# Causal attention of row b placed between the experts of row b-1, and the loop over rows written out

## The reference, cut to what matters

```python
xn = layernorm(x)
# s: causal attention 1, 16 heads of 8
pressure = where(causal, -10000, q1 @ k1.T * hd**-0.5)
attn = 1 - tanh((pressure - threshold) / tau)**2
attn = attn / (sum(attn) + 1e-6)
s = (attn @ v1) @ Wo1.T
# g: attention 2 (softmax, not causal) with residual, then a mixture of 8 experts, top 2, and a shared one
h = rmsnorm(xn, norm1_w);  X = xn + (softmax(q2 @ k2.T * scale) @ v2) @ wo
h2 = rmsnorm(X, norm2_w)
combine = top2 softmax weights of softmax(h2 @ router_w)
moe = swiglu(h2, shared) + sum_e combine[e] * swiglu(h2, expert e)
out = x + s * silu(X + moe)
```

## Time and profile before

| what | value |
|---|---|
| median of 3 runs | 1255.82 us (1254.42 to 1259.35) |
| the profiled execution, its own time | 1256.73 us |
| its span | 1255.0 us |
| PE busy | 1120.9 us, 89% of the span |
| DVE, ACT, POOL busy | 840.3, 649.3, 338.4 us |
| mean granted clock of PE | 0.946 of full |
| first score product | 77.8 us |

### The profile page before, as it was taken

The page is one execution under the profiler, slowest core; times in us unless marked ns, Lnnn a source line. Parts: engine busy times, 40 slices in busy tenths (PEclk is TensorE's granted clock), DMA queues, the critical chain, the costliest instruction groups (busy, mean ns, idle before and its releaser), DMA issues.

```text
span 1255.0 us, 21105 instructions
## 1 busy us (share of the span) xinstructions
PE 1120.9 (89%) x7112; PEld 480.4 (38%) x7112; DVE 840.3 (67%) x1692; ACT 649.3 (52%) x873; POOL 338.4 (27%) x177
## 2 busy tenths in 40 slices
PE   2479999899998899899998999989999899998998
PEld 1112454234541354314543245422464234542365
DVE  6365976569657686576865688655976558656673
ACT  4039821597117861278513883149721597218841
POOL 5400443015420334103341035310543014420013
PEclk8559999799998999989998999989999799999999
DMA  5520432003411135102341033410342104400020
GB/s 173 99 35 2 77 103 42 28 2 77 118 26 28 24 55 134 22 17 44 70 107 28 2 63 99 58 28 2 77 109 35 29 4 74 130 15 18 1 69 8
DMA packets 67970, 66.86 MB, mean 53 GB/s; under 512 B 7760, under 2 KB 59216, under 8 KB 67728
## 3 DMA queue, kind: packets, MB, share of 16 engines
q1 hardware_dynamic: 65088, 61.26, 22.9%
q10 hardware_dynamic: 2768, 4.06, 0.9%
HBM read 50.22 MB, written 14.81 MB: 52 GB/s over the span
## 4 chain that ended last, share of the span: by engine, by line
PE 65%; issue 10%; ACT 10%; DVE 9%; DMA 3%; SPq 2%; POOL 1%; ACTq 1%; DVEq 0%; POOLq 0%
PE M L906 12%; PE O L980 10%; PE O L964 10%; PE S L996 8%; PE S L998 5%; PE S L997 5%; PE S L939 4%; ACT PT L525 4%; DVE PT L676 4%; DVE nmax L639 3%; PE M L1069 1%; SPq L321 1%; PE M L899 1%; PE M L893 1%; PE M L918 1%
## 5 line engine op out<-in xcount | busy, mean ns | idle before, releaser
L525 ACT ACTIVATE PT<-S 128x1024 f32<-128x1024 f32 (+1 forms) x448 | 421.1, 973 | 122.7 <-PE S L939 119.6
L639 DVE TENSOR_REDUCE nmax<-M 128x1 f32<-128x512 f32 x512 | 338.3, 688 | 200.1 <-PE M L906 196.6
L676 DVE SCALAR_TENSOR_TENSOR PT<-PT 128x768 f32<-128x768 f32 (+1 forms) x192 | 215.7, 1173 | 95.9 <-ACT PT L525 95.6
L906 PE MATMUL M<-stackK,stackQ 48*128 48x512 bf16 x512 | 214.5, 434 | 60.9 <-DMA stackK<-scrK 27.5
L964 PE MATMUL O<-PT,V 128*12 128x256 f32 (+3 forms) x2816 | 250.7, 437 | 0.0
L559 ACT ACTIVATE PT<-S 128x1024 f32<-128x1024 f32 x72 | 73.9, 1026 | 313.0 <-PE S L998 313.0
L400 POOL TENSOR_TENSOR split<-split,parts 128x512 f32<-128x512 f32 x32 | 93.1, 2909 | 489.3 <-ACT parts L486 489.3
L415 POOL TENSOR_TENSOR PT<-PT,CB 128x1024 f32<-128x1024 f32 x56 | 132.8, 2373 | 336.3 <-DMA CB<-scrC 171.1
L939 PE MATMUL S<-stackQ,stackK 64*128 64x512 bf16 (+3 forms) x1024 | 205.6, 362 | 18.8 <-DMA stackQ<-mTZ 9.3
L906 PEld LDWEIGHTS M<-stackK,stackQ 48*128 48x128 bf16 x512 | 46.9, 95 | 299.3 <-issue 175.6
L980 PE MATMUL O<-PT,wdn 128*128 128x512 f32 x288 | 151.5, 625 | 0.0
(11 more groups left out here) (174 smaller groups left out, 932.7 us busy)
## 6 DMA issues: line engine op xcount, KB each, us to landing
CB<-scrC SPq DMA_DIRECT2D x64, 256.0 KB, 5.4
stackQ<-scrQ SPq DMA_DIRECT2D x192, 64.0 KB
stackK<-scrK SPq DMA_DIRECT2D x192, 64.0 KB
scrQ<-parts SPq DMA_DIRECT2D x16, 384.0 KB, 4.5
scrK<-parts SPq DMA_DIRECT2D x16, 384.0 KB, 8.3
PT<-in_w_gu ACTq DMA_DIRECT2D x2, 1152.0 KB, 8.2
xin<-in_x SPq DMA_DIRECT2D x8, 256.0 KB, 2.9
xres<-in_x SPq DMA_DIRECT2D x8, 256.0 KB, 3.3
```

The lines of the kernel that those rows point to most:

```text
L525: a.activation(PT[:, n % SLOTS, 2 * q * w:2 * q * w + 2 * w].rearrange("p (r n) -> p r n", r=2), S[k][:, :].rearrange("p (r n) -> p r n", ...
L639: v.tensor_reduce(nmax[:, h % 2, h // 2, t:t + 1], M[k][:, :], AX.X, ALU.max, negate=True).then_inc(m_read[k], 1)
L676: v.scalar_tensor_tensor(p, p, 1.0, p, ALU.subtract, ALU.mult).then_inc(weighed, 1)
L906: t_.matmul(M[k][:, :], stack["Q2"][a:a + ROW_ADD, hp, t * 128:t * 128 + 128], stack["K2"][a:a + ROW_ADD, hp, :], start=True, stop=True).t ...
```

## The change

The program of each row is written out, with no machine loop. One list, ITEMS, gives the order: stage 1 of row b (units 0 to 15), experts 0 to 4 of row b-1, causal units 16 to 19 of row b, experts 5 to 8 of row b-1, units 20 to 23, the gate `G` of row b-1, units 24 to 27. It runs for b from -1 to 8; what belongs to no row is left out, so row 0 has no experts in between and row 7's experts stand alone at the end. BEHIND says which V product (V) or second expert product (D) follows each item. The last two V products of a row lie in units 0 and 1 of the next, its attention-1 output (`oT1`, `ctxT1`, `proj1`) in units 10 to 14.

The maxima X cover head pairs 0 to 2 now, and a run W covers pair 3, in units 0 and 1 of its own row. Its rows in stackQ2 are needed at unit 4. The normalisations' last step, h2lo and the product with sT move from DVE to POOL, the residual addition and cT change engines too. CB holds three routing weights in place of eight. The halves of the V product in stage 1 stay; each stands straight behind its score product.

```diff
-RUNS = {"X": (0, 4), "Y": (4, 6), "Z": (6, 8)}
+RUNS = {"X": (0, 3), "W": (3, 4), "Y": (4, 6), "Z": (6, 8)}
...
-spread(MAX["Y"], {0: 1, 1: 4, 2: 4, 3: 4, 4: 3})
-spread(MAX["Z"], {4: 1, 5: 3, 6: 4, 7: 4, 8: 4})
...
+ITEMS = ([("U", n) for n in range(N1)]
+         + [("E", e) for e in range(5)] + [("U", N1 + u) for u in range(4)]
+         + [("E", e) for e in range(5, NE)] + [("U", N1 + u) for u in range(4, 8)] + [("G", 0)]
+         + [("U", N1 + u) for u in range(8, 12)])
...
+BEHIND |= {("U", 0): ("V", UNITS - 2), ("U", 1): ("V", UNITS - 1),
+           ("E", 0): ("V", N1 - 2), ("E", 1): ("V", N1 - 1), ("E", 2): ("D", 0), ("E", 3): ("D", 1), ("E", 4): ("D", 2),
...
+place_maxima("W", 0, four(0, 1))
+place("U", 2, 0, 0, "maxT_W")
+place_maxima("Y", 0, four(2, 3, 4, 5))
...
+place("U", 12, 1, 1, "xnT")
+place("U", 12, 2, 1, "hT")
+place("U", 13, 1, 1, "Q2")
...
+place("U", 14, 1, 1, "K2")
...
+place_maxima("X", 1, [("E", 3, 1, 2), ("E", 4, 1, 2), ("U", 16, 1, 1), ("U", 17, 1, 1), ("U", 18, 1, 1), ("U", 19, 1, 1),
...
+place("U", 20, 2, 1, "maxT_X")
+place("U", 21, 2, 1, "Q1")
+place("U", 23, 2, 1, "K1")
...
+                if 0 <= b < B:
...
+                        scores_done(b - 1, UNITS - 1)
+                    for name in ("Q1", "K1"):
+                        load_stack(b, name)
+                    maxima_rows(b, "W")
+                if b >= 1:
+                    spread_weights(b - 1)
+                if 0 <= b < B:
+                    maxima_rows(b, "Y")
+                    maxima_rows(b, "Z")
+                if b < B - 1:
+                    for name in ("Q2", "K2"):
+                        store_parts(b + 1, name)
...
+                        scores_done(b, N1 - 1)
+                    for name in ("Q2", "K2"):
+                        load_stack(b + 1, name)
...
+            for b in range(-1, B + 1):
+                if b < B - 1:
+                    norm_apply(b + 1)
+                    split_steps(b + 1, "Q2")
+                    split_steps(b + 1, "K2")
...
-            first_scores(0)
-            with pe.Fori(0, B - 1) as it:
-                row(LOOP.row(it), it, True)
-            row(LAST, B - 1, False)
+            for b in range(-1, B + 1):
+                for item in ITEMS:
+                    kind, n = item
+                    if kind == "U" and 0 <= b < B:
+                        for run, (p0, _p1) in RUNS.items():
+                            if n == NT * (p0 // 2):
+                                pe.wait_ge(row_in[run], (b + 1) * 64)
```

More of the change, by code:

```diff
@@ L88 @@
[L88 to L116, removed]
@@ L119, with four @@
[L119 to L130, removed]
+    assert at == len(MAX[run])
+def four(*units):
+    return [("U", n, i, count) for n in units for i, count in ((0, 1), (1, 1), (2, 2))]
+place_maxima("W", 0, four(0, 1))
+place("U", 2, 0, 0, "maxT_W")
+place_maxima("Y", 0, four(2, 3, 4, 5))
@@ new lines @@
+place("U", 6, 0, 0, "maxT_Y")
+place_maxima("Z", 0, four(6, 7, 8, 9))
+place("U", 10, 0, 0, "maxT_Z")
+place("U", 10, 1, -1, ("oT1", 0))
+place("U", 10, 2, -1, ("oT1", 1))
+place("U", 11, 1, -1, ("oT1", 2))
+place("U", 11, 2, -1, ("oT1", 3))
+place("U", 12, 0, 0, "V1")
+place("U", 12, 1, 1, "xnT")
+place("U", 12, 2, 1, "hT")
+place("U", 13, 1, 1, "Q2")
+place("U", 13, 2, -1, "ctxT1")
+place("U", 14, 1, 1, "K2")
+place("U", 14, 2, -1, "proj1")
+place("E", 2, 0, 1, "V2")
+place("E", 2, 2, 0, ("oT2", 0), ("oT2", 1))
@@ new lines, with rows_of, works @@
+place("U", 20, 2, 1, "maxT_X")
+place("U", 21, 2, 1, "Q1")
+place("U", 23, 2, 1, "K1")
+place("U", 25, 2, 0, "combT")
+place("U", 26, 2, -1, "outT")
+def rows_of(b):
+    for item in ITEMS:
+        yield item, b + (item[0] == "U") - 1
+def works(b, item, i):
+    return [(b + ahead, name) for ahead, name in PLACES[item, i] if 0 <= b + ahead < B]
+M_USE, S_USE, O_USE = {}, {}, {}
+for b in range(-1, B + 1):
+    for item in ITEMS:
+        kind, n = item
+        if kind == "U" and 0 <= b < B or kind == "E" and 0 <= b - 1 < B:
+            S_USE[(b if kind == "U" else b - 1, *item)] = len(S_USE)
+        for i in range(3):
+            for work in works(b, item, i):
+                M_USE[work] = (len(M_USE) % 2, len(M_USE) // 2)
+    for bank, uses in enumerate(([(b, 0), (b, 2), (b - 1, "Y")], [(b, G) for G in (1, 3, 4, 5, 6, 7)])):
+        for r, G in uses:
+            if 0 <= r < B:
+                O_USE[r, G] = (bank, sum(k == bank for k, _c in O_USE.values()))
@@ new lines, in _ @@
+            tau()
+            act.wait_ge(n_in, 32)
+            for b in range(-1, B + 1):
+                for item in ITEMS:
+                    kind, n = item
+                    if kind == "U" and 0 <= b < B:
+                        weights(b, n, 0)
+                    if kind == "E" and b >= 1:
+                        expert(b - 1, n)
+                    for r, name in works(b, item, 0):
+                        take(r, name)
+                    if kind == "U" and 0 <= b < B:
+                        weights(b, n, 1)
+                    for i in (1, 2):
+                        for r, name in works(b, item, i):
+                            take(r, name)
+                    if item in OUTS:
+                        r = b - 1 if OUTS[item] == 2 * NG - 1 else b
+                        if 0 <= r < B:
+                            acc_out(r, OUTS[item])
+                    if kind == "G" and b >= 1:
+                        gate(b - 1)
+                    if 0 <= b < B:
+                        if item == ("U", 16):
+                            squares(b)
+                        elif item == ("U", 20):
+                            router_exps(b)
+                        elif item == ("U", 22):
+                            router_gap(b)
```

1048 lines of the change are left out of this document (486 added, 562 removed), and 4 rows, old and new, of the table BEHIND.

## The result

| kernel | median us | runs, from and to | ratio to the kernel before, 95% |
|---|---|---|---|
| before | 1255.1 | 4, 1253.7 to 1259.4 | 1 |
| changed | 1501.9 | 4, 1487.4 to 1506.3 | 1.194 (1.185 to 1.203) |

What follows compares the result with a forecast made beforehand. TensorE was busy 1120.9 of 1255.0 us, so other engines mattered where it waits. Terms -50 - 8 - 8 + 86 + 25 + 28 + 9 = +82 on 1256.7 gave 1339, forecast as 1338 us; range for 8 in 10 runs 1240 to 1375.

Steps and rivals of the forecast that it cites:

- Rows W: At unit 4 PE waits for rows queued behind the Q1 and K1 loads: 7 us a row, 12 in row 0; +86.
- Stacks Q2 and K2: Maxima X wait for both loads: +1 a row in rows 1 to 7, 15 plus 3.6 in row 0; +25.
- DVE in lumps: In units 20 to 27, units 16 to 19 and expert 5, DVE trails PE; net +3.5 in each of 8 rows, +28.
- Units with four maxima at 2.64 us: Units 0 to 3 were costed at 2.64 us each, plus about 0.5 for whole V products: 11.1 us.
- Edges, -50: At row ends 19.7 us of jumps, 5.4 of drains and 25 of low clock go; -50.
- Clock, 3.6 us for each fall: Behind a row's edge or a long wait, eleven microseconds at the low clock cost 3.6 us for each fall.
- Head, -8: Before row 0, eight maxima and V1 leave and the K load has no stores beside it; together -8 us.
- Tail, +9: Row 7's attention-1 output, copies and proj1 lie beside no other work: 5 us, with 3.6 for the clock; +9.
- Row 0: Two waits were told: 12 us for the rows W and 15 on the stacks, each plus 3.6 for the clock.
- 1 fell: Rival: at unit 4 the rows W are not late and the change is faster, 1240 us between 1252 and 1224; chance 0.18.
- 2 is half right: Rival: ACT's table loads stand between scores at experts 0 and 5, unit 20 and the gate; 41 us, 1379; chance 0.09.
- 3 fell: Rival: the written-out program comes late from memory, 3.3 us gaps at many places; 1400 to 1600 us; chance 0.03.

Runs made afterwards that it cites:

- e2: Changed kernel with only SP's order changed: rows W before the load of Q1, rows Y before that of K1, rows Z behind it; 1426.4 us.
- e3: Changed kernel with the first four maxima X moved from experts 3 and 4 to units 16 to 19, two in each; 1446.6 us.
- e11: Changed kernel with e1, e2, e8, units 16 to 19 ahead of expert 2, and X as four maxima in each of experts 3 to 8; 1330.6 us.
- e1: Changed kernel with the maxima of units 0 to 9 placed two behind each score product instead of 1, 1 and 2; 1487.5 us.
- e4: Changed kernel with the edits of e1, e2 and e3 together; 1369.6 us, ratio 1.087.
- e5: Kernel before with only its machine loops over the rows written out on all five engines, order and waits unchanged; 1239.4 us.
- e6: e4 with the transposes of the maxima of W, Y and Z moved behind the second half of their unit; 1371.9 us.
- e7: e4 with the gate's silu written as sigmoid and copy on ACT plus one more product on POOL; 1382.7 us.
- e8: e4 with POOL's subtractions for wgu_lo moved from the end of the head to row 0, behind the split of K2; 1363.7 us.

## Why the prediction failed, step by step

- **Rows W, +86: right in place, nearly in size.** Eight waits, 43 us where 61 were told, and at most 75 us with what hangs on them (e2). The clock is 0.50 behind them, as told. The mean wait is 5 us in rows 1 to 7 and not 7. It follows the length of the pair Q1 and K1: 1.0 us in row 4 where the pair took 13, 9.8 in row 7 where it took 22, and 18.6 was assumed.
- **Stacks Q2 and K2, +25, of which +7 in rows 1 to 7: the step that failed first.** "Three experts stand in between and cover nearly all: I take +1 (ends 0 and 4)." They cover 15.6 us, and the pair took 24.3, not 18.6: the waits are 9 us a row, and 55 us in all went with them and with the third of row 0's wait that e3 also took. The two numbers of the working were not even set against each other: 18.6 less three experts already leaves 3. And the 18.6 was scaled from a single load, where the trace before held a pair of 21.8. Row 0's wait was 21.8 us, not 15.
- **DVE in lumps, +28: right engine, wrong place.** I looked for it beside the causal products, where TensorE waited only 1.8 us in 3 gaps for DVE's PT. It is where run X is squeezed into the second group of experts: some 33 us by e11, a part of which is row 0's wait on the stacks. Even places in units 0 to 9 gave 14 us, which is not clear of the noise (e1).
- **Units with four maxima at 2.64 us: the second step that failed.** "Four units at the 2.64 us of rows 4." The four units from `maxT_Y` to `maxT_Z` take 15.1 us and took 10.6: 36 us over eight rows there alone. The traces show what fills them, 2.6 us more of gaps a row and 3.7 us at the low clock. The prediction had the clock fall in a row only behind the wait for the rows W, but without that wait (e4) it stays low there for 5.1 us. Whether the new places of the V halves, which were put at nothing, add to this was not tried by itself.
- **Edges, -50: too large, as far as could be tried.** Written-out rows alone give 17 us (e5), where the same terms without the drain had said 45. I paid the whole low clock to the jump, and the clock falls behind the drain's 0.88 us, which the kernel e5 keeps, too. What the drain's end gave in the changed kernel was not tried by itself.
- **Clock, 3.6 us for each fall: counted once a row, and read at one of the longest.** The fall of the earlier trace rows lasts some 14 us; four of the seven last 7 or less. In the changed kernel it falls several times a row, behind waits of little over 1 us as well. What the short falls cost apart from their waits no run shows by itself (e6 changed both).
- **Head, -8: half of it.** The first scores came at 73.8, 4 us earlier than in the earlier trace rows; but POOL's subtractions behind them cost 10 us, which no step had.
- **Tail, +9: right.** From the last V product to the first expert 7.2 us.
- **Row 0.** Only two waits were told there. It is still 30 us too long in e11, which has neither the W wait nor the long one on the stacks: TensorE's gaps in it are 32.0 us there and 10.5 before, of which 9.0 are for nmax and 5.1 for causal products beside POOL's subtractions. That it has all of DVE's work of a row and no experts to hide it is argued.
- **Rivals.** 1 fell (the rows W are late). 2 is half right: the gate's two loads hold TensorE 3.0 us a row, but taking them away brings DVE forward (e7). 3 fell (e5).

What stays open: the last 73 us of e11's span over before, by part 1 at the start, 30 in row 0, 24 in rows 1 to 7 and 19 at the end, were not taken apart further by runs. The trace of e11 names the largest wait that is new in its rows 1 to 7, 24 us for ACT's PT (before 5), with six gaps of 2.98 in unit 24 behind the gate, which e7 could exchange but not remove. That the rest is the price of a row 0 without experts and an end of experts only is argued, not shown.

## What to carry to other kernels

When an order interleaves two rows, write for each stretch the sums of every engine, not only of the one that is busiest over the span: a stretch in which the second engine has more work than the first costs the difference. Here moving run X into six experts that stand together was worth 6 us a row. Set every transfer chain's length beside the cover in the same line, and take the length from the nearest chain of the same kind. Check that a unit keeps its time when its jobs change places. And put small transfers that somebody waits for ahead of large ones on a queue: one new order of the same issues on SP was worth 75 us here.

## What the runs showed of the hardware

- **DVE and POOL.** Small DVE steps on SBUF stood still for the whole of a POOL product: 4.49 and 4.95 us in place of 0.17 (e8). DVE's reductions, which read PSUM, kept 0.67 to 0.69 us in the whole run, beside POOL's products too. It came back when the subtractions met other work: in e11 four causal products lasted 12.07 us, where row 1 needs 4.2 for the same four (2.36 and 1.83), beside POOL's two products of 11 us together.

```profile
136.36 12.07 DVE L710 SCALAR_TENSOR_TENSOR PT<-PT 128x1024 f32<-128x1024 f32 x4 [20.48 <-ACT PT L563]
```
```profile
134.58 11.04 POOL L451 TENSOR_TENSOR wgu_lo<-EX,wgu_hi 128x2304 fp32r<-128x2304 f32 x2
```

  The Trainium skill ("SBUF — State Buffer", "Who interferes with whom") says that the port pair that the two share is an exclusive lock for a whole instruction, that a DVE cast can take it, that a DVE operation with two SBUF inputs contends with a POOL product that reads SBUF, and that a reduction never does. The traces agree in all of these: the cast 4.49 us, the two-input step 4.95, the reductions unchanged.
- **The queue.** Four transfers of 1 KB behind 24 of 64 KB released TensorE only once these had ended, at 1321.1, and ahead of them they kept nobody waiting (e2). The rule of the Trainium skill that the prediction weighed ("DMA: Bandwidth & Descriptors") agrees; the variant that small ones slip past is out.
- **The same loads at two rates.** The pair Q1 and K1 ended 13 us after its start in rows 2 and 4 and 22 us in rows 1 and 7, at the same share of busy DMA engines. A window of row 2, to set beside that of the pair Q2 and K2 in row 4 above (0.58, 77 GB/s):

```profile
435.00:440.00 5.00, 4.08 (x36) 0.93 (x36) 3.80 (x8) 3.67 (x6) 0.00 (x0) 1.00 0.56 146
```

  The cause was not tried. With the shorter pair of row 4 the wait on mTW is 1.0 us, with the longer one of row 7 it is 9.8.
